# A selective-scan layer and soft mixture of experts: reversed sums read from PSUM, SiLU as one ScalarE function, y summed by fp32 transposes

## Chip, cores, metric

One Trainium2 chip, one core. The metric is the device time of one execution in microseconds (us), the median of the runs shown.

## The reference

16 sequences of 512 positions and 256 features, everything fp32. Two selective scans (forward on xf, backward on xb) with 512 inner channels and 16 states, a gate, a projection and a layer norm, then soft routing to 16 experts of 64 slots each.

```python
xf, res = split(x @ in_proj_w.T)
xf = silu(conv(xf, conv_w) + conv_b)
xb = silu(conv(xf, conv_b_w) + conv_b_b)
# for each direction, with u = xf or xb:
delta, B, C = split(u @ x_proj_w.T)
dt = softplus(delta @ dt_proj_w.T + dt_proj_b)
dA_cum = exp(reversed cumsum over l of dt[l+1:] * A)
xs = cumsum(dt * u * B * dA_cum) / (dA_cum + 1e-12)
y = (einsum('bldn,bln->bld', xs, C) + u * D) * silu(res)
x = layernorm(x + (y_f + y_b) @ out_proj_w.T)
# then: logits of 1024 slots, softmax over positions (dispatch) and over slots
# (combine), experts gelu(slots@Wg+bg)*(slots@Wu+bu)@Wd+bd, layernorm(x + combine @ eout)
```

## The kernel before

Three stages follow each other: `sequence_stage` (a loop over the 16 sequences), `expert_stage` and `merge_stage`. The change touches only the first.

A tile is 128 inner channels, 512 positions, one state of one direction. One sequence has 2 directions x 2 pairs of channel chunks x 16 states x 2 chunks = 128 tiles, handled in 64 steps of two tiles; t is the tile, i = t // 2 the step. Each step passes through every engine:

- ScalarE (`decay`, L782) writes e = exp(A dt) of the next step to the PSUM tile `e_ps` (two steps deep) and (`guard`, L792) f = tanh of the reversed sum `rsum` times A/2 plus a constant, which together with a later (1 + f) stands for the reference's division by dA_cum + 1e-12.
- GpSimd (`inputs`, L628) forms g = dt u B two steps ahead in `g_ring` (three slots), and (`times_c`, L637) v = z C in `v_ring` for the steps that aren't in `ON_DVE`.
- VectorE scans (L976, `tensor_tensor_scan`, state = e state + g, in place in `e_ps`, backwards for direction 1), forms z = (1 + f) e (L989) and, for every fourth step (`ON_DVE`, 16 of 64), v itself (L998) in `v_own`.
- TensorE (`add_state`, L1141) adds v to y in the PSUM tile `y_ps` by a matmul with the identity, Y_LAG = 10 tiles later; `SKIPS` adds u D by matmuls with diagonal matrices. Twice per sequence VectorE multiplies y by the gate (`y_gate`, L959).
- SP issues the loads of the rows of B and C, broadcast from DRAM, and the stores.

All other work of a sequence is cut into side slots, written out by hand in `timetable` and placed at tiles by `slot_tiles` from `EARLIEST` and the weights `HOLD`: in0 and res (input projection), conv0/conv1 (convolutions as matmuls with diagonals), x0/x1 (B, C and delta), dt0/dt1 (softplus), out, xnT, rows, cols and so on (logits and softmax of the sequence before). TensorE fills one of two PSUM banks of `side` at the slot's tile, and waits first until the bank's last user is done (`side_free`); `side_step` of ScalarE and VectorE take it up 2 to 5 tiles ("lag") later. Each engine works in its program order. Slots in `AHEAD` belong to the next sequence.

For a conv slot ScalarE writes x/2 (L701) and, in place in the bank, tanh(x/2) (L703); VectorE multiplies u = (tanh + 1) x/2 (L901). For a pair of dt slots ScalarE applies softplus twice (L715, L717), which frees the banks; then VectorE sums both chunks backwards by one scan over 1023 elements (L917), with a tensor `border` of ones and one zero that separates the chunks, and GpSimd forms dt u (L610) and cuts the border (L617).

## Time and profile before

| | |
|---|---|
| median of 3 runs | 6011.23 us (6009.21 to 6022.2) |
| the profiled execution | 6041.35 us, span 6039.5 us |
| mean granted TensorE clock | 0.925 |
| instructions | 50725 |

Engines are PE (TensorE), PEld (its weight loads), DVE (VectorE), ACT (ScalarE), POOL (GpSimd) and SP. A row of lines reads: line, engine, operation, out<-in, shapes, count | busy us, mean ns of one | idle time of the engine before them, by releaser. In the timeline a bracket gives the idle time before an instruction and what ended it. In the windows each engine's busy us (and count) stand in the order PE, PEld, DVE, ACT, POOL, then the granted clock, the DMA share and GB/s. A fp32 matmul is held in the trace as two instructions, a transpose as one.

### The profile page before, as it was taken

The numbers are of one execution on the slowest core, as the hardware profiler recorded it, in microseconds if no ns is written. First come the engines' busy times: TensorE is split into PE (matmuls) and PEld (weight loads), VectorE is DVE, ScalarE is ACT, GpSimd is POOL, SyncE is SP. The second block draws the span as 40 slices with busy tenths as digits, with TensorE's granted clock in tenths as the row PEclk, the third lists the DMA queues.
The fourth block names the chain that finished last, engine by engine and source line by source line (L and its number), as shares of the span: only waits on it lengthen the run. The fifth ranks groups of instructions, "written<-read, shape, count | busy, mean of one in ns | idle before, by whom it ended". The sixth has DMA issues, their size and how long they took to land. (4 is left out here: it accounts for less than half of the span.)

```text
span 6039.5 us, 50725 instructions
## 1 busy us (share of the span) xinstructions
PE 5055.7 (84%) x14640; PEld 2557.8 (42%) x14640; DVE 4751.8 (79%) x4049; ACT 4091.2 (68%) x6429; POOL 4464.2 (74%) x2134
## 2 busy tenths in 40 slices
PE   5888887888887878888888888888888888999988
PEld 2333333333333333333333333443333434565566
DVE  5998989998989998999999999899999871222233
ACT  3878787878887878787878887878788863111100
POOL 3999999999999999999898999998989970000000
PEclk9999899999999999999999999999999999999988
DMA  2444344444443444444443444343434432323265
GB/s 71 129 127 132 123 129 125 130 123 128 128 132 123 129 127 126 126 126 129 124 132 124 128 127 133 126 128 124 132 124 128 130 106 83 101 76 101 80 228 203
DMA packets 555572, 755.29 MB, mean 125 GB/s; under 512 B 124059, under 2 KB 272411, under 8 KB 553245
## 3 DMA queue, kind: packets, MB, share of 16 engines
q1 hardware_dynamic: 555293, 752.04, 39.8%
q8 instruction: 117, 1.92, 0.1%
q14 instruction: 162, 1.33, 0.1%
HBM read 662.04 MB, written 89.82 MB: 124 GB/s over the span
## 5 line engine op out<-in xcount | busy, mean ns | idle before, releaser
L628 POOL TENSOR_TENSOR g_ring<-dtu,b_ring 128x1024 f32<-128x1024 f32 x1026 | 2514.5, 2454 | 362.2 <-DVE e_ps L976 335.1
L976 DVE TENSOR_TENSOR_SCAN e_ps<-e_ps,g_ring 128x1024 f32<-128x1024 f32 x1024 | 2345.2, 2290 | 168.3 <-ACT e_ps L782 156.2
L782 ACT ACTIVATE e_ps<-dt,a_neg 128x512 f32<-128x512 f32 x2050 | 1398.5, 682 | 721.7 <-DVE v_own L998 484.6
L1141 PE MATMUL y_ps<-v_ring,ident 128*128 128x512 f32 x3088 | 1632.2, 638 | 231.9 <-DVE res_gate L959 193.8
L637 POOL TENSOR_TENSOR v_ring<-z_ring,c_ring 128x1024 f32<-128x1024 f32 x768 | 1822.2, 2373 | 0.0
L792 ACT ACTIVATE f_ring<-rsum,consts,a_neg_half 128x512 f32<-128x512 f32 x2050 | 1645.8, 803 | 0.8
L989 DVE SCALAR_TENSOR_TENSOR z_ring<-f_ring,e_ps 128x1024 f32<-128x1024 f32 x768 | 934.9, 1217 | 49.7 <-issue 1.7
L1141 PEld LDWEIGHTS y_ps<-v_ring,ident 128*128 128x128 f32 x3088 | 592.6, 206 | 884.9 <-issue 815.3
L1141 PE MATMUL y_ps<-v_own,ident 128*128 128x512 f32 x1028 | 535.4, 616 | 0.0
L1074 PE MATMUL side<-u,conv_diag 128*128 128x512 f32 x1088 | 491.8, 595 | 23.2 <-ACT disp_ring L743 18.7
L1251 ACT ACTIVATE x_act<-x_gate,x_bg 128x512 f32<-128x512 f32 x128 | 87.9, 687 | 570.8 <-PE x_gate L1283 570.8
L1265 DVE SCALAR_TENSOR_TENSOR x_hT<-x_up,x_bu,x_act 128x512 f32<-128x512 f32 x128 | 96.1, 751 | 373.9 <-PE x_up L1287 373.9
L1106 PE MATMUL side<-seT,xnT 128*128 128x512 f32 x544 | 288.7, 658 | 89.7 <-ACT xnT L720 84.6
L1126 PE MATMUL side<-dispT_ring,xn 128*128 128x128 f32 x2176 | 288.5, 290 | 74.6 <-ACT dt L715 42.5
L1065 PE MATMUL side<-xT_t,w_in 128*128 128x512 f32 x528 | 269.9, 642 | 92.3 <-DVE x L892 50.4
L998 DVE TENSOR_TENSOR v_own<-e_ps,c_ring 128x1024 f32<-128x1024 f32 x256 | 312.7, 1221 | 38.9 <-DMA c_ring<-bc_scr 32.8
L1126 PEld LDWEIGHTS side<-dispT_ring,xn 128*128 128x128 f32 x2176 | 277.3, 203 | 154.3 <-ACT dt L715 69.0
L989 DVE SCALAR_TENSOR_TENSOR e_ps<-f_ring,e_ps 128x1024 f32<-128x1024 f32 x256 | 313.6, 1225 | 19.8 <-ACT f_ring L792 0.5
L1074 PEld LDWEIGHTS side<-u,conv_diag 128*128 128x128 f32 x1088 | 203.3, 189 | 295.7 <-issue 245.9
L1141 PEld LDWEIGHTS y_ps<-v_own,ident 128*128 128x128 f32 x1028 | 197.5, 200 | 234.8 <-issue 234.0
L1395 PE MATMUL m_acc<-m_eo,m_pT 128*128 128x256 f32 x1024 | 242.4, 402 | 64.7 <-DMA m_rinv<-rinv_scr 64.7
L917 DVE TENSOR_TENSOR_SCAN rsum<-dt,border 128x1023 f32<-128x1023 f32 x65 | 269.4, 4144 | 0.0
(134 smaller groups left out, 5206.1 us busy)
## 6 DMA issues: line engine op xcount, KB each, us to landing
b_ring<-bc_scr SPq DMA_DIRECT2D x1027, 256.0 KB, 3.7
c_ring<-bc_scr SPq DMA_DIRECT2D x1025, 256.0 KB, 3.4
pT_scr<-rowT_ring SPq DMA_DIRECT2D x136, 256.0 KB, 4.0
m_pT<-pT_scr SPq DMA_DIRECT2D x16, 2048.0 KB, 8.7
sT_scr<-sT_ring SPq DMA_DIRECT2D x272, 64.0 KB, 2.9
x_xT<-sT_scr SPq DMA_DIRECT2D x16, 1024.0 KB, 9.2
eo_scr<-x_eo SPq DMA_DIRECT2D x32, 512.0 KB, 5.1
m_eo<-eo_scr SPq DMA_DIRECT2D x16, 1024.0 KB, 11.0
```

The lines of the kernel that those rows point to most:

```text
L628: pool.tensor_tensor(g_ring[:, k], dtu[d][:], both(b_ring[:, k:k + 1]), ALU.mult).then_inc(g_done, 1)
L637: pool.tensor_tensor(v_slot(i), z_ring[:, k], both(c_ring[:, k:k + 1]), ALU.mult).then_inc(v_pool, 1)
L782: act.activation(e_ps[:, i % 2, h], dt[d][:, h], ACT.Exp, scale=a_neg[:, d, c, n:n + 1]).then_inc(e_done, 1)
L792: act.activation(f_ring[:, i % FR, h], rsum[d][:, h], ACT.Tanh, scale=a_neg_half[:, d, c, n:n + 1], bias=guard_bias).then_inc(f_done, 1)
L976: dve.tensor_tensor_scan(e, e, g, 0.0, ALU.mult, ALU.add).then_inc(scan_done, 1)
L989: dve.scalar_tensor_tensor(out=z, in0=f_ring[:, i % FR], scalar=1.0, in1=e_ps[:, i % 2], op0=ALU.add, op1=ALU.mult).then_inc(z_done, 1)
L998: dve.tensor_tensor(v_slot(i), e_ps[:, i % 2], both(c_ring[:, k:k + 1]), ALU.mult).then_inc(v_dve, 1)
L1065: mm = pe.matmul(bank, w_in[:, k, m * P:(m + 1) * P], xT_t[:, k], start=(k == 0), stop=(k == KM - 1))
L1074: mm = pe.matmul(bank, conv_diag[:, d, i, k], src[:, i, k:k + L], start=(k == 0), stop=(k == KC - 1))
L1106: mm = pe.matmul(bank, xnT[:, k, t * P:(t + 1) * P], seT[:, k, h * HS:(h + 1) * HS], start=(k == 0), stop=(k == KM - 1))
L1126: mm = pe.matmul(bank[:, k * P:(k + 1) * P], xn[:, t, k * P:(k + 1) * P], dispT_ring[:, i % 2, t * P:(t + 1) * P], start=(t == 0), stop=(t ...
L1141: pe.matmul(y_ps[:, t % 2], ident[:], v, start=(t % (TILES // PAIRS) < 2), stop=True, skip_group_check=True).then_inc(v_used, 1)
```

## The change

- The reversed sums: ScalarE writes softplus to dt and a second time in place into the two side banks; VectorE runs one scan per chunk over 511 elements, with the bank as data and a broadcast column of ones as the factor, and frees the bank. GpSimd's dt u waits for `dt_done`, its cut no longer for the sum and comes two tiles earlier.
- SiLU of the convs: one ScalarE function from the bank to u for the two slots of a pair, after the second is filled. VectorE's product goes, and a conv bank is free after ScalarE.
- `ON_DVE` takes 18 of 64 products with C instead of 16, `v_ring` has 5 slots instead of 6.
- y is summed with positions on the partitions: `add_state` is four 128-column transposes of v that accumulate in `y_ps`, the skips are four matmuls with u as the stationary operand. res is formed in the same layout. Four new side slots yT0 to yT3 transpose the gated y back (`ygT`, ScalarE copies) for `out`.
- The order has the new slots, norm and epilogue start later (tile 24 for 19, 36 for 31), HOLD has other weights.

```diff
     order = """
-        dt1_0 dt1_1 out0 out1 res0 res1 res2 res3 xnT0 xnT1
+        dt1_0 dt1_1 yT0 yT1 out0 yT2 yT3 out1 res0 res1 res2 res3 xnT0 xnT1
...
-HOLD = {"out": 3, "res": 4, "conv0": 4.5, "conv1": 4.5, "x0": 3, "x1": 3, "dt0": 2, "dt1": 2, "in0": 3,
-        "xnT": 2, "rows": 3, "cols": 4, "rowsT": 2, "colsT": 2, "slots": 3}
-STATS_TILE, VAR_TILE, ROUGH_TILE, RSTD_TILE, APPLY_TILE = 19, 22, 24, 26, 29
-EARLIEST = {("dt1", 0): 1, ("out", 0): 12, ("xnT", 0): APPLY_TILE + 2, ("dt0", 2): 36, ("dt1", 2): 66, ("in0", 2): 79,
+HOLD = {"out": 3, "res": 4, "conv0": 2.5, "conv1": 2.5, "x0": 3, "x1": 3, "dt0": 3, "dt1": 3, "in0": 3,
+        "xnT": 2, "yT": 2.5, "rows": 3, "cols": 4, "rowsT": 2, "colsT": 2, "slots": 3}
+STATS_TILE, VAR_TILE, ROUGH_TILE, RSTD_TILE, APPLY_TILE = 24, 27, 29, 31, 34
+EARLIEST = {("dt1", 0): 1, ("yT", 0): 12, ("xnT", 0): APPLY_TILE + 2, ("dt0", 2): 40, ("dt1", 2): 66, ("in0", 2): 79,
...
     FR = 2
-    VR = 6
+    VR = 5
...
     G_AHEAD, B_AHEAD, C_AHEAD = 2, 3, 1
-    SP_LAG, X_STEP = 4, 19
+    SP_LAG, X_STEP = 4, 20
     CUT, A_LEAST = 1e25, 1e-22
-    DTU_LAG, RSUM_LAG, CUT_LAG = 4, 4, 7
-    ON_DVE = [i for i in range(STEPS) if i % 4 == 1]
+    DTU_LAG, RSUM_LAG, CUT_LAG = 4, 4, 5
+    ON_DVE = [i for i in range(STEPS) if i % 7 in (1, 4)]
...
                 d, i = int(TABLE[s][0][-1]), TABLE[s][1]
-                for j in (s - 1, s):
-                    pool.wait_ge(side_free[at.bank(j)], at.freed(j))
+                pool.wait_ge(dt_done, at.pair(s))
...
                 d = int(TABLE[s][0][-1])
-                pool.wait_ge(rsum_done, at.pair(s))
...
                 pool.wait_ge(z_done, b * STEPS + (i + 1 + CR))
-                pool.wait_ge(v_used, b * TILES + (2 * (same_slot_before(i) + 1) + CR))
-                pool.tensor_tensor(v_slot(i), z_ring[:, k], both(c_ring[:, k:k + 1]), ALU.mult).then_inc(v_pool, 1)
+                pool.wait_ge(v_used, 2 * (same_slot_before(b * STEPS + i) + 1) + CR)
+                pool.tensor_tensor(v_slot(b * STEPS + i), z_ring[:, k], both(c_ring[:, k:k + 1]), ALU.mult).then_inc(v_pool, 1)
...
                 d = int(kind[-1]) if kind[-1] in "01" else None
-                if lag == (3 if kind in ("conv0", "conv1") else 2) and kind not in ("out", "cols"):
+                if lag == 2 and kind not in ("out", "cols"):
...
                         act.activation(res_gate[:, i], src, ACT.Tanh).then_inc(tanh_done, 1)
-                    elif kind in ("conv0", "conv1"):
-                        bias = b_conv_half[:, d, i:i + 1]
-                        act.activation(u[d][:, i, PAD:], src, ACT.Identity, scale=0.5, bias=bias).then_inc(half_done, 1)
-                        act.wait_ge(half_done, at.nth(s, ("conv0", "conv1")))
-                        act.activation(src, src, ACT.Tanh, scale=0.5, bias=bias).then_inc(tanh_done, 1)
+                    elif kind in ("conv0", "conv1") and i % 2 == 1:
+                        for j in (0, 1):
+                            act.activation(u[d][:, i - 1 + j, PAD:], side[:, at.bank(s - 1 + j)], ACT.Silu,
+                                           bias=b_conv[:, d, i - 1 + j:i + j]).then_inc(side_free[at.bank(s - 1 + j)], 1)
...
-                        act.activation(dt[d][:, 0], side[:, at.bank(s - 1)], ACT.Softplus).then_inc(
-                            side_free[at.bank(s - 1)], 1)
-                        act.activation(dt[d][:, 1], src, ACT.Softplus).then_inc(free, 1)
+                        for j in (0, 1):
+                            ins = act.activation(dt[d][:, j], side[:, at.bank(s - 1 + j)], ACT.Softplus)
+                        ins.then_inc(dt_done, 1)
+                        act.wait_ge(dt_done, at.pair(s))
+                        for j in (0, 1):
+                            bank = side[:, at.bank(s - 1 + j)]
+                            ins = act.activation(bank, bank, ACT.Softplus)
+                        ins.then_inc(plus_done, 1)
+                    elif kind == "yT":
+                        act.activation(ygT[:, i % 2], src.rearrange("p (c l) -> p c l", c=KI), ACT.Copy).then_inc(free, 1)
...
-                    dve.wait_ge(tanh_done, at.nth(s, ("conv0", "conv1", "res")))
+                    dve.wait_ge(tanh_done, at.nth(s, ("res",)))
...
                                              op0=ALU.add, op1=ALU.mult).then_inc(free, 1)
-                if kind in ("conv0", "conv1") and lag == 4:
-                    d = int(kind[-1])
-                    dve.wait_ge(tanh_done, at.nth(s, ("conv0", "conv1", "res")))
-                    dve.scalar_tensor_tensor(out=u[d][:, i, PAD:], in0=src, scalar=1.0,
-                                             in1=u[d][:, i, PAD:], op0=ALU.add, op1=ALU.mult).then_inc(free, 1)
...
-                        for j in (s - 1, s):
-                            dve.wait_ge(side_free[at.bank(j)], at.freed(j))
-                        sums, steps_ = halves(rsum[d]), halves(dt[d])
-                        last = 2 * L - 1
-                        dve.memset(sums[:, last:] if d == 0 else sums[:, 0:1], 0.0)
-                        out, data, turn = (sums[:, 0:last], steps_[:, 1:], border[:]) if d == 0 else (
-                            sums[:, 1:], steps_[:, 0:last], border[:])
-                        if d == 0:
-                            out, data, turn = out[:, ::-1], data[:, ::-1], turn[:, ::-1]
-                        dve.tensor_tensor_scan(out, data, turn, 0.0, ALU.add, ALU.mult).then_inc(rsum_done, 1)
+                        dve.wait_ge(plus_done, at.pair(s))
+                        for j in (0, 1):
+                            bank, sums = side[:, at.bank(s - 1 + j)], rsum[d][:, j]
+                            out, data = (sums[:, 0:L - 1], bank[:, 1:L]) if d == 0 else (sums[:, 1:L], bank[:, 0:L - 1])
+                            if d == 0:
+                                out, data = out[:, ::-1], data[:, ::-1]
+                            dve.tensor_tensor_scan(out, one.broadcast_to([P, L - 1]), data, 0.0,
+                                                   ALU.mult, ALU.add).then_inc(side_free[at.bank(s - 1 + j)], 1)
+                        dve.memset(rsum[d][:, :, L - 1:L] if d == 0 else rsum[d][:, :, 0:1], 0.0).then_inc(rsum_done, 1)
...
-                for i in (2 * p, 2 * p + 1):
+                for i in (2, 3):
...
                 dve.wait_ge(v_used, b * TILES + ((TILES // PAIRS if p == 0 else 0) + CR))
-                pair = slice(2 * p, 2 * p + 2)
-                dve.tensor_tensor(yg[:, pair], y_ps[:], res_gate[:, pair], ALU.mult).then_inc(y_gated, 1)
+                cols = slice(2 * p * P, (2 * p + 2) * P)
+                sums = y_ps[:].rearrange("p h (t d) -> p (h t) d", d=2 * P)
+                dve.tensor_tensor(yg[:, :, cols], sums, res_gate[:, :, cols], ALU.mult).then_inc(y_gated, 1)
...
                     dve.wait_ge(c_loaded[k], b * (RING.count(k) * 16) + (RING[:i].count(k) + 1) * 16)
-                    dve.wait_ge(v_used, b * TILES + (2 * (same_slot_before(i) + 1) + CR))
-                    dve.tensor_tensor(v_slot(i), e_ps[:, i % 2], both(c_ring[:, k:k + 1]), ALU.mult).then_inc(v_dve, 1)
+                    dve.wait_ge(v_used, 2 * (same_slot_before(b * STEPS + i) + 1) + CR)
+                    dve.tensor_tensor(v_slot(b * STEPS + i), e_ps[:, i % 2], both(c_ring[:, k:k + 1]), ALU.mult).then_inc(v_dve, 1)
...
+            def rows_of(lb, q):
+                return y_ps[:, lb // 2, (lb % 2 * 2 + q) * P:(lb % 2 * 2 + q + 1) * P]
...
                 pe.wait_ge(side_free[at.bank(s)], at.freed(s, 0))
-                if kind in ("in0", "res"):
-                    if kind == "in0" and i == 0:
+                if kind == "in0":
+                    if i == 0:
                         pe.wait_ge(xT_loaded, at.seq(s) * 16 + 16)
-                    m = i if kind == "in0" else KI + i
                     for k in range(KM):
-                        mm = pe.matmul(bank, w_in[:, k, m * P:(m + 1) * P], xT_t[:, k], start=(k == 0), stop=(k == KM - 1))
+                        mm = pe.matmul(bank, w_in[:, k, i * P:(i + 1) * P], xT_t[:, k], start=(k == 0), stop=(k == KM - 1))
+                elif kind == "res":
+                    for k in range(KM):
+                        mm = pe.matmul(bank, xT_t[:, k, i * P:(i + 1) * P], w_in[:, k, DI:2 * DI],
+                                       start=(k == 0), stop=(k == KM - 1))
+                elif kind == "yT":
+                    if i == 0:
+                        pe.wait_ge(y_gated, at.seq(s) * 2 + 1)
+                    for c in range(KI):
+                        mm = pe.transpose(bank[:, c * P:(c + 1) * P], yg[:, i, c * P:(c + 1) * P], ident[:])
...
                 elif kind == "out":
-                    if i == 0:
-                        pe.wait_ge(y_gated, at.seq(s) * 2 + 1)
+                    for t in (2 * i, 2 * i + 1):
+                        read("yT", t)
...
                         for c in range(KI):
-                            mm = pe.matmul(bank[:, t % 2 * DM:(t % 2 + 1) * DM], yg[:, c, t * P:(t + 1) * P], w_out[:, c],
+                            mm = pe.matmul(bank[:, t % 2 * DM:(t % 2 + 1) * DM], ygT[:, t % 2, c], w_out[:, c],
...
                         pe.wait_ge(y_gated, b * PAIRS + (t // (TILES // PAIRS) + 1))
-                v = v_slot(i)[:, t % 2]
-                pe.matmul(y_ps[:, t % 2], ident[:], v, start=(t % (TILES // PAIRS) < 2),
-                          stop=True, skip_group_check=True).then_inc(v_used, 1)
+                v = v_slot(b * STEPS + i)[:, t % 2]
+                for lb in range(LT):
+                    mm = pe.matmul(rows_of(lb, t % 2), v[:, lb * P:(lb + 1) * P], ident[:], is_transpose=True,
+                                   start=(t % (TILES // PAIRS) == 0 and lb % 2 == 0), stop=True, skip_group_check=True)
+                mm.then_inc(v_used, 1)
...
-                        pe.matmul(y_ps[:, q], d_diag[:, d, 2 * pair + q], u[d][:, 2 * pair + q, PAD:],
-                                  start=False, stop=True, skip_group_check=True)
+                        for lb in range(LT):
+                            pe.matmul(rows_of(lb, q), u[d][:, 2 * pair + q, PAD + lb * P:PAD + (lb + 1) * P],
+                                      d_diag[:, d, 2 * pair + q], start=False, stop=True, skip_group_check=True)
...
```

## Rows read from the trace of the kernel before

**Rows 1.** The page: busy time, share of the span and instructions of each engine.

```profile
PE 5055.7 (84%) x14640; PEld 2557.8 (42%) x14640; DVE 4751.8 (79%) x4049; ACT 4091.2 (68%) x6429; POOL 4464.2 (74%) x2134
```

**Rows 2.** Windows: one sequence, its last quarter, a stretch with transposes; busy by engine, granted clock.

```profile
2548.70:2853.40 304.70, 250.35 (x696) 117.81 (x696) 278.72 (x200) 245.77 (x387) 277.76 (x133) 0.92 0.42 127
2776.00:2853.00 77.00, 54.82 (x174) 27.50 (x174) 70.70 (x47) 61.31 (x97) 74.16 (x33) 0.89 0.43 125
2651.30:2658.40 7.10, 6.15 (x26) 2.92 (x24) 6.58 (x5) 7.07 (x12) 7.10 (x4) 1.00 0.48 143
```

**Rows 3.** Waits of VectorE in that sequence: us in total, times, longest.

```profile
DVE e_ps L976 <- ACT e_ps L782: 9.5, 7, 3.4
DVE col_stats L930 <- PE side L1111: 3.1, 1, 3.1
DVE u L901 <- ACT side L703: 2.6, 3, 0.9
DVE v_own L998 <- DMA c_ring<-bc_scr: 2.3, 1, 2.3
```

**Rows 4.** Waits of GpSimd in that sequence.

```profile
POOL g_ring L628 <- DVE e_ps L976: 23.8, 15, 5.6
```

**Rows 5.** Timeline at the first reversed sum of a sequence: start, us, engine, line.

```profile
2553.39 9.77 DVE L917 TENSOR_TENSOR_SCAN rsum<-dt,border 128x1023 f32<-128x1023 f32 x1
...
2563.24 0.20 POOL L617 TENSOR_TENSOR dt<-consts 128x1 f32<-128x1 f32 x1 [2.22 <-DVE rsum L917]
```

**Rows 6.** The line of the reversed sum: durations ns min/median/max, first and last start.

```profile
L917 DVE TENSOR_TENSOR_SCAN rsum<-dt,border x65: 2282/3148/10147, 92.5 to 4896.1; 128x1023 f32<-128x1023 f32 x65
```

**Rows 7.** Lines of the whole span, shapes apart.

```profile
L976 DVE TENSOR_TENSOR_SCAN e_ps<-e_ps,g_ring 128x1024 f32<-128x1024 f32 x1024 | 2345.2, 2290 | 168.3 <-ACT e_ps L782 156.2 <-POOL g_ring L628 10.4
L637 POOL TENSOR_TENSOR v_ring<-z_ring,c_ring 128x1024 f32<-128x1024 f32 x768 | 1822.2, 2373 | 0.0
L792 ACT ACTIVATE f_ring<-rsum,consts,a_neg_half 128x512 f32<-128x512 f32 x2050 | 1645.8, 803 | 0.8
L1141 PE MATMUL y_ps<-v_ring,ident 128*128 128x512 f32 x3088 | 1632.2, 638 | 231.9 <-DVE res_gate L959 193.8 <-POOL v_ring L637 38.1
L782 ACT ACTIVATE e_ps<-dt,a_neg 128x512 f32<-128x512 f32 x2050 | 1398.5, 682 | 721.7 <-DVE v_own L998 484.6 <-DVE z_ring L989 227.1
L989 DVE SCALAR_TENSOR_TENSOR z_ring<-f_ring,e_ps 128x1024 f32<-128x1024 f32 x768 | 934.9, 1217 | 49.7 <-issue 1.7 <-ACT f_ring L792 0.4
...
L998 DVE TENSOR_TENSOR v_own<-e_ps,c_ring 128x1024 f32<-128x1024 f32 x256 | 312.7, 1221 | 38.9 <-DMA c_ring<-bc_scr 32.8
...
L917 DVE TENSOR_TENSOR_SCAN rsum<-dt,border 128x1023 f32<-128x1023 f32 x65 | 269.4, 4144 | 0.0
...
L901 DVE SCALAR_TENSOR_TENSOR u<-side,u 128x512 f32<-128x512 f32 x136 | 93.0, 684 | 82.8 <-ACT side L703 82.8
...
L701 ACT ACTIVATE u<-side,b_conv_half 128x512 f32<-128x512 f32 x136 | 92.1, 678 | 61.6 <-PE side L1074 61.6
```

**Rows 8.** Timeline at the softplus of dt0_2 and dt0_3.

```profile
2626.50 1.14 ACT L739 ACTIVATE row_t<-row_t,row_stats 128x1024 f32<-128x1024 f32 x1
...
2627.74 1.28 ACT L715 ACT_TABLE_LOAD   x1
...
2629.53 0.59 ACT L717 ACTIVATE dt<-side 128x512 f32<-128x512 f32 x1
...
2630.14 1.28 ACT L782 ACT_TABLE_LOAD   x1
...
2632.16 2.30 DVE L976 TENSOR_TENSOR_SCAN e_ps<-e_ps,g_ring 128x1024 f32<-128x1024 f32 x1 [3.43 <-ACT e_ps L782]
```

**Rows 9.** Timeline of TensorE at the full clock.

```profile
2646.67 3.60 PE L1074 MATMUL side<-u,conv_diag 128*128 128x512 f32 x8
...
2655.59 0.60 PE L1120 MATMUL side<-ident,disp_ring 128*128 128x128 f32 x4
2656.03 1.02 PE L1141 MATMUL y_ps<-v_ring,ident 128*128 128x512 f32 x2
```

18 lines of the change are left out of this document (7 added, 11 removed).

## The prediction

> **What bounds the kernel now.** I read the page first: over the span VectorE and GpSimd are nearly as busy as TensorE [rows 1]. The shares mix stages, so I took the windows of one turn of the loop over sequences, from one VectorE gate (L959) to the next: 304.7 us, of which VectorE works 278.7, GpSimd 277.8, TensorE 250.4 and ScalarE 245.8 [rows 2]. There are 16 such turns, 4875 us of the span of 6039.5; the rest (prologue, experts, merge) the edit hardly touches. Two engines over 90% leave the question which of them is waited for last. VectorE's waits in that turn name ScalarE (9.5 us for the exponentials e_ps), TensorE (3.1 for a side bank) and small others [rows 3], and none names GpSimd. GpSimd's name VectorE: 23.8 us for the scan that frees a g_ring slot [rows 4]. So VectorE's queue is the path: its work plus its waits for ScalarE and TensorE make the turn. GpSimd has some 27 us to spare, but acts on VectorE in another way. The reversed sum L917 took 9.77 us at one place, and GpSimd waited its last 2.22 us for that same sum before its cut (L617) [rows 5]. The shortest L917 is 2.28 us, the longest 10.1 [rows 6]; the mean is 4.14 [rows 7]. Its two inputs (dt, border) lie both in SBUF, as GpSimd's do; the scan L976, with one input in PSUM, takes 2.29 for 1024 elements and shows no such stretch.
>
> **What VectorE sheds and takes on, per turn.** (1) The four reversed sums cost 4 x 4.14 = 16.6 us now. After, each is two scans of 511 elements with data in PSUM and one broadcast SBUF column. L976's rate gives 2.29 x 511/1024 = 1.14 each, with a start-up at most 1.2 [rows 7]: 8 x 1.17 = 9.4, so -7.2. Bounds: if they still ran at the SBUF form's mean there would be 0; if every stall was as in [rows 5] only once a turn, the sum is what the mean says, so no more than -7.5. (2) The eight SiLU products L901 go: 8 x 0.68 = -5.5. (3) Two more products with C come over (18 for 16): 2 x 1.22 = +2.4; GpSimd loses 2 x 2.37 = 4.7, which nothing waits for. Sum: -10.3 us.
>
> The Trainium skill (SBUF — State Buffer, "Who interferes with whom") says that a tensor_tensor with both inputs in SBUF contends with GpSimd's reads, the second comer being blocked fully. The trace agrees in that the sum ended 2.1 us after GpSimd had gone idle, which is the length of an undisturbed one, and it differs in that the sum was held for 7.5 us, longer than one GpSimd product of 2.37 [rows 5, 7]. By that rule alone, one product of wait per sum, the edit would take 4 x 2.4 = 9.6 off instead of 7.2.
>
> **What TensorE sheds.** An addition to y is one 512-column fp32 matmul, which the trace holds as two instructions. At the full clock eight such instructions took 3.60 us, 0.45 each with the tail of the last, and four transposes of 128 columns, one instruction each, let the next matmul start after 0.44, 0.11 each [rows 9]. The code adds 128 tiles per turn: 128 x 2 x 0.45 = 115 us now, 128 x 4 x 0.11 = 56 after; the skips in four pieces and the products of res cost the same columns as before; yT adds 16 x 0.11 = 2. TensorE falls from 250 to about 193 us. It is not on the path as such, so I count only the waits that name it: the 3.1 us of col_stats, and, with the one-pass Silu that also frees a conv bank two tiles earlier, the 2.6 of u<-L703 [rows 3], and of the 9.5 for e_ps some 1.2 that stand at the convs, where ScalarE waited for TensorE (61.6 us in 17 sequences) [rows 7]. Sum: -6.9; bounds 0 (they come back at other places) and -9 (with waits of ScalarE that are passed on).
>
> **What ScalarE takes on.** It is 59 us per turn from full, but bursts count. When VectorE begins the scan of one step, ScalarE begins the exponentials of the next: 0.68 + 0.80 + 0.68 = 2.16 us until the second is out, against 2.29 + 1.22 = 3.51 of VectorE [rows 7]. A block of other work in ScalarE is hidden up to 1.35 us (up to 2.2 if it falls behind the second tanh), plus what VectorE does on the side in that step. Check: the softplus block, load, two softplus, load, lasted from 2627.74 to 2631.42, 3.7 us, right behind a row's exponential of 1.14 + 0.19; 5.0 - 1.35 = 3.7, and VectorE waited 3.43 [rows 8]. The rule holds.
>
> The softplus block gets two more passes of 0.59 and a wait for its own result: 3.7 becomes 4.9, three of four stand bare: 3 x 1.2 = +3.6 (bounds 0, +4.8). Silu: nothing in the trace shows the function. Nearest are L701, 0.68, for a pass, and softplus, which needs a load in and a load back of 1.28 [rows 7, 8]. I take the loads: a pair of convs becomes a block of 2 x 1.28 + 2 x 0.68 = 3.9 in place of two separate ones of 1.34. Less 1.35 to 2.2 of room and 0 to 1.2 of VectorE's side work, 0.5 to 2.5 are bare; I take 1.6: 4 x 1.6 = +6.4 (bounds 0, if Silu needs no load, and 15.6, with no room at all). Copies of yT: 0.59 each, within the room, 0; their cover gone, +2.4.
>
> The dt pair holds both side banks until VectorE's scans (lag 4 instead of 2). At dt0_3 (tile 41) the next fill is in0_0 (42), whose ScalarE pass is due at 44, while the bank comes free at 45; at dt1_3 (68) the same with slots2. TensorE's queue holds additions behind that fill, ScalarE's the next exponentials. Two places at 1 us: +2 (bounds 0, +6). The ring of five: step i reuses the slot of step i - 7 (one place i - 6) instead of i - 8, and TensorE adds five steps late, so a margin of two steps stays; 0 while TensorE keeps up, which it does better than before. The later norm (tiles 24 to 34) packs the epilogue from tile 36; its end at 122 doesn't move. POOL's queue: the cut no longer waits for the sum, its 2.2 us [rows 5] fall to an engine with slack. SP's queue keeps its order; only the side stores move by tiles. c_ring's DMA wait of 2.3 [rows 3] stays.
>
> **Sum.** -10.3 - 6.9 + 3.6 + 6.4 + 2 = -5.2 us per turn, x 16 = -83; the epilogue has four transposes' copies more, +2. The profiled execution would go from 6041.35 (span 6039.5, 1.9 around it) to 5960. The median of the runs is 6011.2, 0.5% below it; from there: 5930.
>
> **Rivals.** *Silu is cheap or TensorE's relief is larger.* If Silu is in the table set of exp and tanh, 6.4 falls away: -11.6 x 16 = -186, 5825; with every ScalarE block hidden, -17.2 x 16, 5735. For it: tanh and exp alternate without loads. Against: softplus doesn't. 0.17. 
>
> *Nothing lasting.* GpSimd works 74.2 of 77 us in the last quarter of the turn [rows 2]: there, VectorE's gains are bounded by GpSimd, whose 12 products per 7 steps replace 7 per 4 (3.98 us per step for 4.06). If the first three quarters return theirs in ScalarE's blocks, the time stays at about 6010. 0.13.
>
> *Slower: ScalarE's blocks have no room.* Where blocks fall in steps that already carry a wait, their whole length lands on VectorE: Silu 15.6, softplus 4.8, dt banks 6: +26.4 against 17.2 shed, +9.2 x 16 = +147, 6160. It decides from blocks of more than 17.2 us bare per turn. Against: the check above, where room was there. 0.15.
>
> *Slower: the clock.* After the edit 512 transposes per turn do what matmuls did. If they didn't hold TensorE's clock at 2.4 GHz, its 193 us would become 386 at 1.2, over the turn by 81: 16 x 81, about 7310. In the trace a stretch of 7.1 us with 16 transposes among 26 instructions kept the full clock [rows 2], but matmuls stood between them. 0.05. The Trainium skill (TensorE: Matmul & The Clock Gate, "Part 4: PE-mode transpose") says that transposes don't count as busy in the way matmuls do, which speaks for this rival.
>
> **Numbers.** Likeliest, its own range 5860 to 5985: 0.50. With the rivals, faster by over 0.2% (12 us, what this kernel's runs can tell): 0.50 + 0.17 = 0.67; the same 0.13; slower 0.20. Range 5760 to 6060: from most of Silu without loads to half of the bare blocks; left out are the clock, the upper half of the blocks' case and every block hidden.
>
> **What would show it.** Right: reversed sums of 1.1 to 1.2 us x 2, none longer beside GpSimd; additions of 4 x 0.11; TensorE near 200 us a turn; a load before and after each Silu pair; turns near 299.5 us; VectorE's waits for e_ps risen from 9.5 to about 20, those for col_stats and u gone. Wrong: no load at Silu; granted clock far below 0.92; waits for side banks behind dt pairs over 3 us; VectorE waiting for GpSimd's g_ring or v_ring over the whole turn.

## The result and the profile after

| | before | after |
|---|---|---|
| median | 6010.22 us (6003.52 to 6022.2) | 6292.24 us (6287.11 to 6294.45) |
| span of the profiled execution | 6039.5 us | 6291.8 us |
| mean granted TensorE clock | 0.925 | 0.838 |

The ratio is 1.0466, 95% interval 1.0448 to 1.0484: slower by 4.7%. The prediction (5930 us, range 5760 to 6060, slower 0.20) was wrong in sign and range.

The page of the changed kernel, busy time of each engine, against [rows 1]:

```profile
PE 4545.2 (72%) x19796; PEld 3058.0 (49%) x19796; DVE 4614.6 (73%) x4006; ACT 4270.7 (68%) x6620; POOL 4289.3 (68%) x2102
```

TensorE, VectorE and GpSimd all do less, ScalarE 180 us more, and the kernel takes longer. The window of the same turn, from gate to gate, against [rows 2]:

```profile
2530.40:2847.90 317.50, 220.16 (x1017) 149.59 (x1016) 268.62 (x197) 257.14 (x399) 267.43 (x130) 0.81 0.39 122
```

VectorE works 268.6 us for 278.7, which is -10.1 where the prediction had -10.3. Yet the turn lasts 317.5 for 304.7: 48.9 us without work for 26.0. All 16 turns together, from the first gate to the last, before and after:

```profile
124.10:4957.30 4833.20, 4020.75 (x11132) 1892.06 (x11132) 4408.85 (x3159) 3919.05 (x6157) 4435.28 (x2105) 0.92 0.41 127
128.80:5198.20 5069.40, 3507.93 (x16252) 2384.53 (x16252) 4277.45 (x3126) 4096.75 (x6346) 4261.21 (x2073) 0.81 0.39 121
```

In the mean of the turns VectorE's work falls by 8.2 us (275.6 to 267.3), two less than in the turn above, and its time without work rises by 23.0 (26.5 to 49.5). VectorE's waits in that turn (us, times, longest), against [rows 3]:

```profile
DVE e_ps L971 <- ACT e_ps L786: 26.2, 9, 4.5
DVE res_gate L954 <- PE y_ps L1149: 7.9, 2, 4.0
DVE x L892 <- PE side L1099: 5.3, 2, 3.1
DVE v_own L993 <- DMA c_ring<-bc_scr: 2.5, 1, 2.5
DVE col_stats L924 <- PE side L1118: 2.5, 3, 1.9
DVE row_stats L915 <- ACT row_t L727: 2.2, 2, 1.9
```

The wait for ScalarE's exponentials rose from 9.5 to 26.2 us, and two waits are there that the turn before did not have: at the gate (7.9 us) and for x, the sum of x and the projected y (5.3). GpSimd in that turn, against [rows 4]:

```profile
POOL g_ring L626 <- DVE e_ps L971: 33.5, 14, 9.7
POOL g_ring L626 <- PE y_ps L1149: 12.2, 5, 4.5
```

GpSimd waits more too, so it isn't the bound. What ended VectorE's largest waits is seen in the timeline of a Silu pair:

```profile
2560.59 1.28 ACT L699 ACT_TABLE_LOAD   x1
...
2562.26 1.22 DVE L984 SCALAR_TENSOR_TENSOR z_ring<-f_ring,e_ps 128x1024 f32<-128x1024 f32 x1
...
2563.02 1.27 ACT L699 ACTIVATE u<-side,b_conv 128x512 f32<-128x512 f32 x2 [1.14 <-PE side L1081]
...
2564.30 1.28 ACT L786 ACT_TABLE_LOAD   x1
...
2565.60 0.69 ACT L786 ACTIVATE e_ps<-dt,a_neg 128x512 f32<-128x512 f32 x1
...
2567.64 2.30 DVE L971 TENSOR_TENSOR_SCAN e_ps<-e_ps,g_ring 128x1024 f32<-128x1024 f32 x1 [4.15 <-ACT e_ps L786]
```

The load is there, as taken in the prediction, and a wait stands behind it that was not: the pair is run when its second slot has been filled, and ScalarE stands 1.14 us for that. The block lasts from 2560.59 to 2565.60, 5.0 us and not 3.9. This pair waits longer than the mean: over the span the wait inside is 50.1 us for 136 passes (L699 below), 0.7 us a pair. The end of the turn, at dt1_2 and dt1_3, against [rows 8]:

```profile
2831.45 1.28 ACT L713 ACT_TABLE_LOAD   x1
...
2832.75 1.08 ACT L713 ACTIVATE dt<-side 128x512 f32<-128x512 f32 x2
2833.86 1.07 ACT L718 ACTIVATE side<-side 128x512 f32<-128x512 f32 x2
...
2834.95 1.28 ACT L786 ACT_TABLE_LOAD   x1
...
2836.97 2.30 DVE L971 TENSOR_TENSOR_SCAN e_ps<-e_ps,g_ring 128x1024 f32<-128x1024 f32 x1 [4.53 <-ACT e_ps L786]
...
2839.18 2.30 DVE L909 TENSOR_TENSOR_SCAN rsum<-consts,side 128x511 f32<-128x511 f32 x2
...
2840.42 3.77 PE L1133 MATMUL side<-dispT_ring,xn 128*128 128x128 f32 x16 [9.67 <-DVE rsum L909]
...
2847.86 1.23 DVE L954 TENSOR_TENSOR res_gate<-y_ps,res_gate 128x1024 f32<-128x1024 f32 x1 [3.97 <-PE y_ps L1149]
```

The block lasts 4.8 us as predicted (4.9). Then a chain that the prediction priced at 1 us: VectorE is late by the block, so its two sums are, so the side banks are, and TensorE, which wants the bank for slots2, stands 9.67 us with the additions to y behind it in its queue. The gate needs these, and VectorE waits 3.97 for them. Lines of the whole span, shapes apart, against [rows 7] (TensorE's wait behind the reversed sums is in the second):

```profile
L1149 PE MATMUL y_ps<-ident,v_ring 128*128 128x128 f32 x5920 | 950.2, 303 | 290.9 <-DVE res_gate L954 238.9 <-POOL v_ring L635 52.0
...
L1133 PE MATMUL side<-dispT_ring,xn 128*128 128x128 f32 x2176 | 343.3, 324 | 317.5 <-DVE rsum L909 308.0 <-ACT u L699 5.5 <-ACT dispT_ring L732 4.0
...
L909 DVE TENSOR_TENSOR_SCAN rsum<-consts,side 128x511 f32<-128x511 f32 x130 | 150.3, 1198 | 56.3 <-ACT side L718 56.3
...
L699 ACT ACTIVATE u<-side,b_conv 128x512 f32<-128x512 f32 x136 | 86.1, 685 | 50.1 <-PE side L1081 49.8
L699 ACT ACT_TABLE_LOAD x65 | 83.4, 1283 | 7.4 <-PE side L1081 6.3
```

The sums take 1.20 us each (1.17 predicted), and TensorE's wait behind them at this line is 308 us in 16 turns.

Below, a version's time per turn is measured from its first gate to its last, 32 gates and 16 turns later (the starts of y_gate in its trace). It is 302.1 us before (124.1 to 4957.3) and 316.8 after (128.8 to 5198.2): +14.7, in 16 turns 236 of the 252 us by which the two profiled executions differ. (The medians differ by 282: the profiled execution before was 0.5% above its median.) All ratios are to the kernel before, timed on the same chip. The times per turn come from one execution of each version, on several chips; the kernel before had medians from 6010 to 6045 us on them, so a difference of two such times is good to about 1 us, an estimate (35 us in 16 turns are 2.2 at the most).

### The profile page after: what moved, and what is told of

It is laid out like the page before. It is cut to its first block and busy times, and to the rows that moved or that the text cites. A ratio compares the mean times of both kernels' runs of the same rounds, so it can differ in the third digit from the quotient of the medians.

```text
span 6291.8 us, 61028 instructions
## 1 busy us (share of the span) xinstructions
PE 4545.2 (72%) x19796; PEld 3058.0 (49%) x19796; DVE 4614.6 (73%) x4006; ACT 4270.7 (68%) x6620; POOL 4289.3 (68%) x2102
## 5 line engine op out<-in xcount | busy, mean ns | idle before, releaser
L626 POOL TENSOR_TENSOR g_ring<-dtu,b_ring 128x1024 f32<-128x1024 f32 x1026 | 2420.3, 2363 | 768.0 <-DVE e_ps L971 588.9
L635 POOL TENSOR_TENSOR v_ring<-z_ring,c_ring 128x1024 f32<-128x1024 f32 x736 | 1736.0, 2360 | 26.3 <-issue 26.0
L1149 PE MATMUL y_ps<-ident,v_ring 128*128 128x128 f32 x5920 | 950.2, 303 | 290.9 <-DVE res_gate L954 238.9
L1149 PEld LDWEIGHTS y_ps<-ident,v_ring 128*128 128x128 f32 x5920 | 803.7, 159 | 603.1 <-issue 480.6
L1133 PE MATMUL side<-dispT_ring,xn 128*128 128x128 f32 x2176 | 343.3, 324 | 317.5 <-DVE rsum L909 308.0
L1133 PEld LDWEIGHTS side<-dispT_ring,xn 128*128 128x128 f32 x2176 | 322.5, 235 | 336.8 <-DVE rsum L909 315.6
L1149 PE MATMUL y_ps<-ident,v_own 128*128 128x128 f32 x2312 | 370.1, 297 | 0.2 <-DVE res_gate L954 0.2
L1149 PEld LDWEIGHTS y_ps<-ident,v_own 128*128 128x128 f32 x2312 | 305.2, 156 | 127.2 <-issue 127.2
L1099 PE MATMUL side<-w_out,ygT 128*128 128x256 f32 x544 | 195.0, 537 | 156.6 <-ACT ygT L721 156.6
L1063 PE MATMUL side<-xT_t,w_in 128*128 128x512 f32 x272 | 169.9, 759 | 129.1 <-DVE rsum L909 101.9
```

Of the source, the lines that this page charges most:

```text
L626: pool.tensor_tensor(g_ring[:, k], dtu[d][:], both(b_ring[:, k:k + 1]), ALU.mult).then_inc(g_done, 1)
L635: pool.tensor_tensor(v_slot(b * STEPS + i), z_ring[:, k], both(c_ring[:, k:k + 1]), ALU.mult).then_inc(v_pool, 1)
L1133: mm = pe.matmul(bank[:, k * P:(k + 1) * P], xn[:, t, k * P:(k + 1) * P], dispT_ring[:, i % 2, t * P:(t + 1) * P], start=(t == 0), stop=(t ...
L1149: mm = pe.matmul(rows_of(lb, t % 2), v[:, lb * P:(lb + 1) * P], ident[:], is_transpose=True, start=(t % (TILES // PAIRS) == 0 and lb % 2 = ...
```

## Experiments

In the rows, and in the text on them, a wait is named by what VectorE's instruction writes: e_ps is the scan, u the convs' product, rsum the reversed sum, res_gate <- PE y_ps the gate, res_gate <- ACT res_gate the gating of res, x the sum of x and out, row_stats and col_stats the statistics of the two softmaxes. A wait per turn is a sixteenth of its total.

**One part undone at a time.** First the old SiLU (L701, L703 and L901 as before, HOLD 4.5), then the old reversed sum, then y by matmul with the old order and norm tiles, each in the changed kernel.

```diff
-                        act.activation(u[d][:, i - 1 + j, PAD:], side[:, at.bank(s - 1 + j)], ACT.Silu, ...
+                        act.activation(u[d][:, i, PAD:], src, ACT.Identity, scale=0.5, bias=bias)
+                        act.activation(src, src, ACT.Tanh, scale=0.5, bias=bias)
```

> The changed kernel with the old SiLU alone (half, tanh and VectorE's product, conv banks held to lag 4, HOLD 4.5). Theory A, the Silu blocks of ScalarE with their two table loads stand bare: in the turn from 2530.4 to 2847.9 us of the changed kernel VectorE's waits before e_ps behind the four Silu pairs are 4.2, 3.3, 2.4 and 4.3 us, 14.2 together; without them, with 5.5 us of products and some 4 us of small conv waits back, a turn loses about 5 us and the time goes to about 6215. Rival B, the side banks held by the reversed sums and the y chain are the cause and ScalarE's blocks only fill waits: within 30 us of 6292.

Measured 1.0311 (1.0291 to 1.0331): undoing SiLU gives back 1.55%.

```diff
-                            dve.tensor_tensor_scan(out, one.broadcast_to([P, L - 1]), data, 0.0, ALU.mult, ALU.add)
+                        dve.tensor_tensor_scan(out, data, turn, 0.0, ALU.add, ALU.mult).then_inc(rsum_done, 1)
```

> The changed kernel with the old reversed sum alone (from dt in SBUF, banks free after ScalarE, no second softplus). Theory B, the banks held for the sum cost more than the faster sum brings: waits of about 2.0, 2.8, 4.0 and part of 4.5 us a turn go, 7 us of contention come back: about -3 us a turn, 6240. Rival A (ScalarE's Silu blocks alone are the cause): the sum's 7 us come back and little goes, about 6390.

Measured 1.0329 (1.0302 to 1.0357): 1.4% back. VectorE's wait at the gate for TensorE falls from 74.8 to 7.8 us in the span, so it belonged to the banks that the sums hold.

```diff
-                for lb in range(LT):
-                    mm = pe.matmul(rows_of(lb, t % 2), v[:, lb * P:(lb + 1) * P], ident[:], is_transpose=True, ...
+                pe.matmul(y_ps[:, t % 2], ident[:], v, start=(t % (TILES // PAIRS) < 2), ...
```

> The changed kernel with y by the 512-column matmul again (no yT slots, gate and out as before, norm and epilogue at their old tiles; ring of five and 18 products stay). Theory C, the transposes leave TensorE at the low clock and the longer chain to out stalls VectorE: the waits of 3.1 and 2.1 us before x and 4.0 before the gate go, about 9 us a turn, 6150, and the granted clock is back above 0.9. Rival: TensorE's relief was a gain that the other parts hide; then TensorE is at 250 us a turn again and the time rises above 6320.

Measured 1.0262 (1.0239 to 1.0286): 2.0% back, at a clock of 0.913, and 311.5 us per turn (129.9 to 5113.3). The part that frees TensorE costs most. Between the gates of the first and the last turn VectorE waits 86.4 us for x in the changed kernel and not at all here, which is 5.4 a turn; the other differences (gate +1.3, work +0.9, e_ps -1.2, the gating of res -1.1) nearly cancel.

**One part alone.** The kernel before with the 18 products and the ring of five, then with y transposed on top of these.

```diff
-    VR = 6
+    VR = 5
-    ON_DVE = [i for i in range(STEPS) if i % 4 == 1]
+    ON_DVE = [i for i in range(STEPS) if i % 7 in (1, 4)]
```

> The kernel before with only 18 products with C on VectorE and the ring of five. If they are harmless, the ratio to the kernel before lies between 0.995 and 1.002, and the 0.8% of the kernel with only y transposed are the transposes'. Rival: the shorter ring or the two products (2.4 us of VectorE a turn) cost it, ratio about 1.008.

Measured 0.9922 (0.9891 to 0.9952), 298.6 us per turn (-3.5; by the ratio of the medians it would be -2.9, an estimate). It is faster than both kernels, though VectorE got two more products, 2.4 us a turn; neither expectation had that. The line of the reversed sum, grouped, and its durations (ns min/median/max, first and last start), in this version:

```profile
L918 DVE TENSOR_TENSOR_SCAN rsum<-dt,border 128x1023 f32<-128x1023 f32 x65 | 192.5, 2961 | 4.6 <-ACT dt L718 4.6
```

```profile
L918 DVE TENSOR_TENSOR_SCAN rsum<-dt,border x65: 2283/2289/7805, 91.4 to 4842.0; 128x1023 f32<-128x1023 f32 x65
```

The median fell from 3148 ns [rows 6] to 2289, the mean from 4144 [rows 7] to 2961. With the products at other steps, half of the sums run undisturbed, and 4 x 1.18 = 4.7 of the 7.2 us that the sums from PSUM were to bring had come without them. An undisturbed sum, and GpSimd's product that begins behind it:

```profile
203.61 2.28 DVE L918 TENSOR_TENSOR_SCAN rsum<-dt,border 128x1023 f32<-128x1023 f32 x1
203.83 4.22 POOL L629 TENSOR_TENSOR g_ring<-dtu,b_ring 128x1024 f32<-128x1024 f32 x1 [0.34 <-DVE e_ps L977]
```

The 64 sums of the loop are of two kinds. Where GpSimd is between two products when the sum begins, the sum takes 2.28 us and the next product 4.2 in place of 2.36. Where a product is under way, the sum is held, by one product or by several. In the kernel before 49 of 64 sums were held (4.75 us in the mean) and 15 weren't; in this version it is 32 (3.66) and 32.

> Old SiLU and old reversed sum, only y by transposes (with 18 products and the ring of five). If theories A and B hold and add up: about 6165. If the transposes (theory C) are all of it: 6290. If they are harmless: 6010 or below.

Measured 1.0081 (1.0062 to 1.0101), 304.1 us per turn: +5.5 over the version without it, where the prediction had -3.1.

Three more versions each add one thing to the version with 18 products. (The last two bring the weights `HOLD` of their part with them, which move some other slots by a tile; that is in their price.) The first moves only the tiles of norm and epilogue, as the four new slots force it:

```diff
-STATS_TILE, VAR_TILE, ROUGH_TILE, RSTD_TILE, APPLY_TILE = 19, 22, 24, 26, 29
+STATS_TILE, VAR_TILE, ROUGH_TILE, RSTD_TILE, APPLY_TILE = 24, 27, 29, 31, 34
-EARLIEST = {... ("dt0", 2): 36, ...
+EARLIEST = {... ("dt0", 2): 40, ...
```

> The kernel before with 18 products, the ring of five, and the norm's tiles of the changed kernel (24 to 34 for 19 to 29, xnT from 36 for 31, dt0_2 at 40 for 36); y by matmul, old SiLU, old sums. It prices the later start that the four new slots force on the order. Theory (packing costs): the version with y transposed alone stood 1.6% above the one without (1.0081 for 0.9922), of which a later x gave back 0.8; if the packed slots hold the rest, this is 1.000 +- 0.003. Rival (packing costs nothing when ScalarE and the banks have room, and the rest of the 1.6% lies in the copies and the two hops from gate to out): 0.992 to 0.994.

Measured 1.0069 (1.0046 to 1.0092), 304.4 us per turn: +5.8, as much as the version with y transposed, without one transpose, and more than the 1.000 that was expected. Its reversed sum, and VectorE's waits from 100 to 5200 us, then the same waits of the version with 18 products:

```profile
L918 DVE TENSOR_TENSOR_SCAN rsum<-dt,border 128x1023 f32<-128x1023 f32 x65 | 219.5, 3377 | 0.0
```

```profile
DVE e_ps L977 <- ACT e_ps L783: 180.1, 80, 3.4
DVE u L902 <- ACT side L704: 89.5, 73, 2.5
...
DVE col_stats L931 <- PE side L1112: 42.1, 19, 4.0
```

```profile
DVE e_ps L977 <- ACT e_ps L783: 144.7, 80, 3.5
...
DVE col_stats L931 <- PE side L1112: 59.7, 19, 4.0
DVE u L902 <- ACT side L704: 39.2, 48, 0.9
...
DVE res_gate L960 <- PE y_ps L1142: 9.1, 2, 8.9
```

The slots from xnT to dt1 lie in 31 tiles (36 to 67) for 35 (31 to 66), and `slot_tiles` puts ten pairs of them on one tile, where there were two. Per turn u waits +3.1, e_ps +2.2, the sums take +1.7 (mean 3377 ns for 2961), col_stats -1.1: 5.9.

With y transposed on top of these same tiles, the same 5.5 stand at other waits. Between the gates VectorE waits 87.8 us for x (5.5 a turn, none here), since four transposes and ScalarE's copies now stand between the gate and out; against it u waits less by 2.3 a turn, col_stats by 1.7, e_ps by 0.9, the gating of res by 0.6. So TensorE's relief is worth up to 5.5 a turn there, and the longer way to x takes it all.

The second adds the sums from the banks:

> The kernel before with 18 products, the ring of five and the reversed sums read from the side banks (two scans of 511, a second softplus into the banks), old SiLU, y by matmul. With the stall beside GpSimd already shrunk by the 18 products (mean 2.96 us a sum), the sums shed only 4 x (2.96 - 2.40) = 2.2 us per turn, the softplus blocks add up to 4.8 and the banks held 2 to 6. Theory (the step is a loss by itself once the stall is gone): 0.992 + 0.010 to 0.020, 1.002 to 1.012. Rival (it only hurts together with Silu and the transposed y): 0.990 to 0.995.

Measured 1.0111 (1.0087 to 1.0135), 305.7 us per turn: +7.1. VectorE's waits, then TensorE's, from 100 to 5200 us:

```profile
DVE e_ps L975 <- ACT e_ps L785: 172.8, 144, 4.0
DVE col_stats L929 <- PE side L1110: 99.3, 35, 4.0
...
DVE res_gate L958 <- PE y_ps L1140: 53.9, 17, 8.9
DVE u L901 <- ACT side L701: 53.4, 48, 1.6
...
DVE rsum L914 <- ACT side L719: 15.3, 32, 0.7
```

```profile
PE side L1125 <- DVE rsum L914: 134.2, 32, 5.0
...
PE side L1064 <- DVE rsum L914: 92.8, 16, 5.8
```

Against the version with 18 products, per turn: the double softplus +1.8 (e_ps) and about +1 (rsum); what waits for TensorE, itself behind the held banks, col_stats +2.5, gate +2.8, u +0.9, together 6.2. VectorE's work fell by 1.7. That the banks are behind these is shown for two of them by the version that undoes the sums (the gate 74.8 to 7.8, col_stats 36.9 to 4.0 us in the span); for u it is read from TensorE's waits.

The third adds Silu:

> The kernel before with 18 products, the ring of five and SiLU as one function on the pair, old sums, y by matmul. VectorE sheds 8 x 0.68 = 5.5 us per turn, ScalarE gets four blocks of 3.9 (5 with the wait for the second fill). Theory (blocks mostly bare, 3.3 each): +13 - 5.5 = +7.7 us per turn, 2%: 1.010 to 1.016. Rival (the blocks cost so much only beside the other parts): 0.990 to 1.000.

Measured 1.0069 (1.0045 to 1.0094), 304.4 us per turn: +5.8, between the two expectations. VectorE's waits:

```profile
DVE e_ps L969 <- ACT e_ps L781: 379.0, 158, 4.7
...
DVE col_stats L923 <- PE side L1104: 10.6, 3, 4.0
```

Per turn e_ps +14.6 against -2.5 of u, -3.1 of col_stats and -4.0 of work (busy time between the gates 4301.6 us for 4364.8): 5.0, and smaller waits make the rest.

The parts add up: 298.6 + 7.1 + 5.8 + 5.5 = 317.0 us per turn for 316.8 measured, and Silu and sums together, which is the version with y by matmul, take 311.5, the sum to the digit. That it fits to the digit is chance. By the ratios of medians the parts make 0.9922 + 0.0189 + 0.0147 + 0.0159 = 1.0417 for 1.0466, as near as their intervals allow (together 0.0075, an estimate). So no large part of the loss needs two of the parts at once; 1 or 2 us a turn may.

**Is it the table, and is it the clock?** In the changed kernel Tanh in place of Silu (another function, so the output is no longer the layer's; it shows only the price of the loads), and, apart from that, a matmul with a zero matrix ahead of each addition.

```diff
-                            act.activation(u[d][:, i - 1 + j, PAD:], side[:, at.bank(s - 1 + j)], ACT.Silu,
+                            act.activation(u[d][:, i - 1 + j, PAD:], side[:, at.bank(s - 1 + j)], ACT.Tanh,
```

> The changed kernel with tanh(x + b) in place of SiLU (so u is another function and the output another; it shows the price of the table loads alone, since tanh needs none beside exp). If the two loads of 1.28 us around each pair are what stands bare: 4 x 2.57 = 10.3 us of ScalarE a turn go, at least 8 of them bare, ratio about 1.025. Rival: the pair's form (both banks wait for the second fill, one long block) costs, not the loads: about 1.04.

Measured 1.0222 (1.0193 to 1.0251), e_ps waits 287 us for 430. Without its loads the block of Silu costs 2.4% less, 9 us per turn: the loads are the price. The wait for the pair's second fill is still there (139.6 us at L699, for 50.1 with the loads ahead of it). By an estimate from both runs (5.8 - 9.2), Silu without loads would be a gain of some 3 us per turn.

```diff
+                pe.matmul(y_ps[:, t % 2, 0:256], nought[:], w_in[:, 0, 0:256], start=False, stop=True, ...
                 for lb in range(LT):
```

> The changed kernel with one added fp32 matmul of a zero matrix with 256 columns per tile, accumulated into y (adds nought to the result), some 57 us of TensorE a turn at the full clock. Theory C (the low clock makes fills late): the granted clock rises from 0.84 to above 0.9, VectorE's waits for x (100 us in all) fall below 50, those at the gate (75 us) too, ratio about 1.035 for 1.047. Rival: TensorE's queue order and the extra hop make them late, not the clock; then the added work makes it slower, above 1.05.

Measured 1.0472 (1.0443 to 1.0502), the clock back at 0.908:

```profile
core 0: 6331.3 us, clock 0.908
```

```profile
DVE e_ps L973 <- ACT e_ps L787: 482.9, 175, 4.6
DVE res_gate L956 <- PE y_ps L1153: 94.0, 16, 6.0
DVE col_stats L926 <- PE side L1120: 70.4, 48, 2.7
DVE x L894 <- PE side L1101: 54.0, 32, 3.2
```

x waits shrink (86 to 54), others grow (gate 75 to 94, col_stats 37 to 70, e_ps 430 to 483), and the ratio is that of the changed kernel: neither 1.035 nor above 1.05, as the two expectations had it. The experiment adds TensorE work with the clock, so it bounds only the sum of both; the version that undoes Silu keeps the clock at 0.837 and gains all the same.

**The banks and the packing.** At least four tiles between a dt pair and the next slot:

```diff
+        if s and table[s - 1][0] in ("dt0", "dt1") and table[s - 1][1] % 2 == 1:
+            tile = max(tile, tiles[-1] + 4)
```

> The changed kernel with the slot after each dt pair placed at least four tiles behind it in the timetable, so that no ScalarE pass is due before VectorE has freed the banks. Theory B (ScalarE waits in order for a fill whose bank VectorE frees later): the waits of TensorE for the sum (308 + 102 us) no longer reach VectorE, some 6 us a turn, ratio about 1.03. Rival: the denser slots between tiles 45 and 75 take it back: 1.045 or more.

Measured 1.0300 (1.0270 to 1.0330), 1.7% less than the changed kernel: VectorE's wait at the gate falls from 74.8 to 7.5 us, TensorE's waits for rsum fall from 435 to 318 us. In this version sixteen pairs of slots between tiles 36 and 73 share a tile, and it is faster all the same. Then x one lag later with the norm two tiles later, in the changed kernel and in the version with y transposed alone:

```diff
-STATS_TILE, VAR_TILE, ROUGH_TILE, RSTD_TILE, APPLY_TILE = 24, 27, 29, 31, 34
+STATS_TILE, VAR_TILE, ROUGH_TILE, RSTD_TILE, APPLY_TILE = 26, 29, 31, 33, 36
-                if kind == "out" and lag == 2:
+                if kind == "out" and lag == 3:
```

> The changed kernel with VectorE's sum of x and out due two tiles later (tile 19 for 17 and 25 for 23), norm and epilogue moved by two tiles with it. Theory: the extra hop yT, ScalarE's copy, out leaves too little time, and VectorE's 86 us of waits for x are bare: ratio about 1.034 for 1.047. Rival: they return at the norm and the epilogue, which are now later still: 1.043 or more.

> Only y transposed (old SiLU, old sum, 18 products, ring of five), x two tiles later. If the hop is all that the transposed y costs over the kernel with 18 products and ring of five alone (0.992): its 102 us of waits for x go, ratio 0.992 to 0.997. If the lower clock costs too: stays at 1.005.

Measured 1.0602 (1.0583 to 1.0621) and 1.0005 (0.9988 to 1.0023): a loss of 1.4% in the one, a gain of 0.8% in the other. To part the two edits, the norm alone two tiles later in the changed kernel:

> The changed kernel with the norm's tiles two later (26 to 36 for 24 to 34, xnT from 38 for 36), x taken as before. It splits the version with x later, which had this and the later x and stood 1.3% above the changed kernel. Theory (the packing behind the norm did it): 1.060 to 1.066. Rival (the later x did it): 1.044 to 1.050.

Measured 1.066 (1.0624 to 1.0696). So in the changed kernel the later norm costs 1.9%, and the later x gives 0.6% of it back. VectorE's waits:

```profile
DVE e_ps L971 <- ACT e_ps L786: 587.3, 184, 6.2
```

All slots from tile 38 to 68 now stand two to a tile, and VectorE waits 587 us for ScalarE's exponentials, for 430. The version with only y transposed and x later has the same pairs without the long blocks of Silu and of two softplus; it waits 212 for them and gained. So the later norm is dear together with these blocks; why on these tiles, and not on those of the version with room after dt, isn't shown. Other repairs: the old SiLU, room after dt and x later together, and the ring of six again.

> The changed kernel with all three theories' repairs: old SiLU, room after the dt pairs, x later. If they are separate costs they add up: 1.047 less 1.55, 1.7 and 1.2% gives about 1.002. If they share waits (VectorE waits once where two blocks fall in one step), it stays above 1.015.

> The changed kernel with six v slots. GpSimd waited 163 us for TensorE there (19 before). If VectorE is the path and GpSimd has slack, nothing moves: ratio within 0.003 of 1.047. Rival: those waits are passed on to VectorE, then 1.04 or less.

Measured 1.0143 (1.0126 to 1.0161): what the first two bring by themselves (1.0466 - 0.0155 - 0.0166 = 1.0145); the later x, bought with the later norm, brings nothing. And 1.0423 (1.0405 to 1.0440): VectorE's list is that of the changed kernel to 5 us a row, so the ring is worth little: 0.4%, with an interval of 0.25 around it, a little more than expected.

**The other way.** The version with 18 products, with the norm two tiles earlier than in the kernel before (17, 20, 22, 24, 27).

> The kernel before with 18 products, the ring of five and the norm's tiles two earlier than before (17 to 27 for 19 to 29, xnT from 29 for 31). Moving them five later cost 1.5% (1.0069 for 0.9922), 5.8 us per turn. Theory (the packing of the slots behind the norm sets this price, and there is still some in the order of before): 0.985 to 0.990. Rival (the slots of before already have room; only a packing to two slots per pair of tiles costs): 0.991 to 0.994. With luck this is the fastest version.

Measured 0.9867 (0.9845 to 0.9890), 296.4 us per turn, the fastest of all:

```profile
DVE e_ps L977 <- ACT e_ps L783: 129.8, 90, 2.4
DVE row_stats L922 <- ACT row_t L724: 1.9, 6, 0.5
```

Between the gates the wait for row_stats, 42.2 us in the version with 18 products, is gone (2.5 a turn), and that for e_ps is smaller by 0.9 a turn.

## Why the prediction was wrong

The bound was read rightly: VectorE's work plus its waits for ScalarE and TensorE make the turn, GpSimd is not on the path. VectorE's work fell by 8.2 us a turn where 10.3 were computed. What failed are the costs of all three large parts: the sum has waits of +5.1 (6.4 + 3.6 + 2 - 6.9) where the time without work rose by 23.0. Two of the prediction's own signs of being wrong were there, a clock of 0.838 and waits behind the dt pairs of over 3 us. Per turn, predicted and measured (the version with one part alone against the one with 18 products; the pattern's saving on the sums counts as the products'):

| part | predicted | measured | off |
|---|---|---|---|
| 18 products, ring | +2.4 | -3.5 | -5.9 |
| sums from the banks | -7.2 + 3.6 + 2 = -1.6 | +7.1 | +8.7 |
| Silu | -5.5 + 6.4 - 3.8 = -2.9 | +5.8 | +8.7 |
| y transposed | -3.1 | +5.5 | +8.6 |
| turn | -5.2 | +14.7 | +19.9 |

**Silu: "I take 1.6: 4 x 1.6 = +6.4 (bounds 0 ... and 15.6, with no room at all)".** Mis-sized: the waits for e_ps rose by 14.6 us per turn, close to the upper bound, 3.7 for each of the four blocks where 1.6 were taken. Two loads and two passes are 3.9 us, and after the load the pair waits for its second fill, 1.14 in the timeline above and 1.2 in the mean of the version with Silu alone (81.7 us at that line, 68 pairs). Of the 5.1 less than a third was hidden. The room rule had been checked at one block only, without a wait inside. The relief of the side banks was real and came with this part: u and col_stats waits fell by 5.6 (5.7 in the sum, which put the 3.1 of col_stats down to the faster TensorE).

**The banks: "Two places at 1 us: +2 (bounds 0, +6)".** Mis-sized: 6.2, if all waits for TensorE that grew are the banks'. I saw that a bank comes free three tiles after the next fill wants it, and took it as slack of the bank. But fills and additions share TensorE's queue, the banks are freed by VectorE, which is late by the softplus block itself, and the gate needs those additions: 9.67 us of TensorE became 3.97 of VectorE in the timeline above. The softplus blocks themselves were right or high (3.6 predicted, about 2.8).

**The sums: -7.2.** The new length was right (1.20), but the old one was a property of the neighbours, not of the form: 4.7 of the 7.2 came with the pattern of the products. Here the Trainium skill (SBUF — State Buffer, "Who interferes with whom") pointed right: by it the delay comes from what GpSimd reads from SBUF at that moment, so it hangs on the neighbour. The trace agrees: with no change of the instruction the median is back at 2289 ns, and in the kernel before and the version with 18 products every sum of the loop that began between two of GpSimd's products took 2.28 or 2.29 us.

**y: "The later norm (tiles 24 to 34) packs the epilogue from tile 36; its end at 122 doesn't move" and "Copies of yT: 0.59 each, within the room, 0".** Both were named and put at nothing. The later tiles alone cost 5.8 us a turn in the version with y by matmul (304.4), and the transposes on top of them nothing more (304.1). But the waits are others. The way from the gate over transpose and copy to x costs 5.5, at x. In the changed kernel too the part's price, 5.4, stands at x. What part of it the later tiles have there isn't shown: its slots share a tile in two places only, not in ten. The copies did not fail by their length but by the hop that they put into the chain.

**TensorE's relief (3.1 of the 6.9).** It works 220 us for 250 in the turn. Its relief was there, up to 5.5 a turn against the version with the tiles moved, and the hop took all of it. In the changed kernel the waits that named TensorE at the gate and at col_stats were waits for its queue behind a bank, not for its speed: with the old sums they fall from 74.8 to 7.8 us and from 36.9 to 4.0.

The rival "ScalarE's blocks have no room" was the nearest, right in sign and mechanism (softplus, Silu, banks) but with 9.2 us per turn for 14.7; it lacked the later tiles, the hop to x and the wait in the pair. The forecast did not miss by one term: three parts fell short by 8.6 to 8.7 us a turn each, and 5.9 came back with the products, 4.7 of it a saving that the sums were to bring. The clock did fall, from 0.925 to 0.838, as the rival on the clock had it, but TensorE isn't the bound, and no sign of 7310 us was seen. The Trainium skill's sentence on transposes (TensorE: Matmul & The Clock Gate, "Part 4: PE-mode transpose") points the same way; no run here parts the transposes from the smaller amount of TensorE's work. The drain beside a load that the Trainium skill gives (ScalarE: Activation LUTs, "What ACT_TABLE_LOAD costs") isn't in the trace: the load at 2564.30 follows the last Silu at 0.01 us.

Open stays how much the lower clock costs by itself, since no version had one without the other; and which slots make the later norm dear, since versions with as many pairs on one tile lost and gained.

## What to carry to other kernels

When two engines hand each other work in every step, a block of other work on the one is paid by the other beyond a room of one step's difference; count the waits inside the block (a pair's second fill, a table load), and don't take a room that one block showed for the room of all. A buffer that is held longer can cost by what stands in the queue behind its next user, not only by its own slack. A new hop in a chain is priced by the chain's end, not by the hop's length. Price the schedule that an edit forces by moving the tiles alone before writing the edit, and price a stall beside another engine by moving the neighbour: these two, a list of steps and five numbers (with a ring of five for six), gave 1.3% here, where the rewrite cost 4.7%.

## What the runs showed of the hardware

- Silu costs a pass of 685 ns per 128x512, as Identity does (678 [rows 7]), and beside Exp a table load of 1283 ns on the way in and on the way back; Tanh in its place takes 685 ns and needs none.
- With y summed by transposes the granted clock falls from 0.925 to 0.838 (0.849 with that part alone), with y by matmul in the same kernel it is 0.913, and 256 columns of zero matmul a tile raise it to 0.908, while the time stays the same within the interval.
- A scan with one operand in PSUM and a broadcast column as the other (L909) ran at 1198 ns on the mean of 130; the sum over both chunks (1023 elements) from two SBUF tensors took 2.28 us where GpSimd was between two products at its start, which then made GpSimd's next product 4.2 us for 2.36, and 2.4 to 10.2 us where a product was under way (64 sums each in the kernel before and in the version with 18 products).
